# Graph attention layer on one core: TensorE's work of a step regrouped by operand type, the output projection's halves two steps apart, and counts of adj taken ahead of its transposes

## The reference

```python
h = max(layernorm(x), 0)                                   # (8, 1024, 64)
q, k, v = (h @ W + b).reshape(b, m, 8, 64)                 # 8 heads
scores = einsum(q, k) / 8 + edge_bias[adj]                 # (8, 8 heads, 1024, 1024)
scores = leaky_relu(scores, 0.2)
scores = where(adj > 0, scores, -1e9)
attn = softmax(scores, axis=-1)
out = einsum(attn, v).reshape(b, m, 512)
return x + out @ Wp + bp
```

## Time and profile before

| what | us |
|---|---|
| median of 3 runs (all: 1156.67, 1154.0, 1156.44) | 1156.44 |
| the profiled execution | 1153.11 |
| its span, first to last instruction | 1151.3 |
| PE busy in it (88%) | 1013.4 |
| DVE busy (81%) | 932.3 |
| ACT busy (67%) | 773.6 |
| POOL busy (42%) | 482.6 |

### The profile page before, as it was taken

How to read it: one execution, slowest core, us unless ns; L and a number is a source line. 1 busy time by engine, 2 the same in 40 slices (tenths; PEclk the granted TensorE clock), 3 DMA queues, 4 the chain that set the end, 5 groups by cost and what they waited for, 6 DMA issues and landing times. The chain is left out here.

```text
span 1151.3 us, 32436 instructions
## 1 busy us (share of the span) xinstructions
PE 1013.4 (88%) x9055; PEld 990.2 (86%) x9055; DVE 932.3 (81%) x3374; ACT 773.6 (67%) x1721; POOL 482.6 (42%) x865
## 2 busy tenths in 40 slices
PE   3247899999999999999989999999989999999996
PEld 3137898999989988989989989999989999899995
DVE  3725888978988879878898879978988789978984
ACT  1336776677767766767766767667777677667762
POOL 1001344444434544444444434444544355444444
PEclk9976999999999999999999999999999999999998
DMA  7183343433343343423434243433434243333220
GB/s 156 29 281 110 88 118 103 127 99 114 114 115 114 95 121 93 138 83 113 122 96 143 76 123 111 117 94 105 129 95 130 81 139 111 109 99 108 75 79 8
DMA packets 193427, 125.53 MB, mean 109 GB/s; under 512 B 34452, under 2 KB 181908, under 8 KB 193236
## 3 DMA queue, kind: packets, MB, share of 16 engines
q1 hardware_dynamic: 190736, 122.73, 37.2%
q10 hardware_dynamic: 2500, 0.55, 0.3%
HBM read 79.19 MB, written 44.04 MB: 107 GB/s over the span
## 5 line engine op out<-in xcount | busy, mean ns | idle before, releaser
L1007 POOL TENSOR_SCALAR a_line<-w,a_bias 128x256 f32<-128x256 f32 x512 | 260.3, 508 | 550.6 <-DVE w L1673 504.2
L1650 DVE CUSTOM_DVE_ANT_0 w<-bank,mask_rows 128x256 f32<-128x256 f32 x512 | 196.6, 421 | 119.3 <-PE bank L1140 96.3
L1426 ACT ACTIVATE pt<-bank 128x512 f32<-128x512 f32 x256 | 154.4, 603 | 183.7 <-PE bank L1150 178.7
L1197 PE MATMUL bank<-pt,nat_sb 128*65 128x128 f32 x2048 | 271.7, 277 | 0.2
L1197 PEld LDWEIGHTS bank<-pt,nat_sb 128*65 128x65 f32 x2048 | 237.4, 141 | 0.6 <-issue 0.6
L1673 DVE SCALAR_TENSOR_TENSOR w<-w,shift,a_line 128x256 f32<-128x256 f32 x512 | 224.1, 477 | 7.0 <-issue 4.9
L1662 DVE TENSOR_TENSOR onehot<-val,counts_to 128x512 fp32r<-128x512 f32 x256 | 175.3, 686 | 9.8 <-DVE val_max L1617 9.2
L1408 ACT ACTIVATE mask_own<-bank,mask_bias 128x512 bf16<-128x512 f32 x256 | 177.1, 692 | 2.1 <-PE bank L1174 2.1
L1150 PE MATMUL bank<-ident,w 128*128 128x128 f32 x1024 | 157.1, 277 | 0.0
L1417 ACT ACTIVATE t_sb<-bank 128x512 fp32r<-128x512 f32 x256 | 152.4, 595 | 4.6 <-PE bank L1162 4.5
L1139 PE MATMUL bank<-t_sb,q_hi 128*128 128x256 f32 x512 | 146.9, 308 | 5.3 <-issue 4.6
(11 more groups left out here) (132 smaller groups left out, 1654.2 us busy)
## 6 DMA issues: line engine op xcount, KB each, us to landing
adj_in<-in_adj_dram SPq DMA_DIRECT2D x64, 512.0 KB, 4.0
mask_store<-mask_own SPq DMA_DIRECT2D x64, 512.0 KB, 3.2
mask_rows<-mask_store SPq DMA_DIRECT2D x512, 64.0 KB, 2.4
stack_store<-stage SPq DMA_DIRECT2D x14, 256.0 KB, 3.1
h_stack<-stack_store SPq DMA_DIRECT2D x7, 512.0 KB, 5.2
h_nl<-nl_store SPq DMA_DIRECT2D x28, 128.0 KB, 3.0
x_res<-in_x_dram SPq DMA_DIRECT2D x16, 128.0 KB, 2.3
nl_store<-nl_rest SPq DMA_DIRECT2D x1, 2048.0 KB, 8.8
```

The source lines that it names most:

```text
L1007: nc.gpsimd.tensor_scalar(a_line[:, i % 2, :], w[:, i, :], 5.0, a_bias[:, i:i + 1], ALU.mult, ALU.add)\
L1197: last = pe.matmul(o_part[0:D + 1, P * u:P * u + P], nat_sb[:, t % 2, p % 4 * 2 + u, k, :], pt[:, p % 2, u, k, :], start=(k == 0), stop=(k ...
L1426: nc.scalar.activation(pt[:, p % 2], turned_bank[:, :].rearrange("p (u k r) -> p u k r", u=2, k=2), ACT.Exp, scale=0.8).then_inc(probs_rea ...
L1650: nc.vector.tensor_tensor_reduce(w[:, i, :], row_bank[:, SLOTS * u:SLOTS * u + SLOTS], mask_rows[:, t % 2, p % 4 * 2 + u, :], 0.25, LEAST_ ...
```

## The change

- The lags: `TURN_A` goes from 5 to 9 (still step 1), `COUNT` from 6 to 7 (step 2 to step 3), `USED` from 7 to 8 (step 3 to step 0), `PROJ` from 27 to 28, with its second half two steps after the first (steps 0 and 2, before 3 and 0), `NORM` from 28 to 29 with the same distance (steps 1 and 3, before 0 and 1), `SUM` from 30 to 32 (step 2 to step 0), `OUT` from 31 to 33.
- PE's step: `project`, `turn_adj` and `count` come right behind `weigh` and ahead of `gather_keys`; before, they came behind `natural`, in the order `turn_adj`, `count`, `project`. The wait for `adj_ready` moves from `turn_adj` to `count`, which is now the first reader of a tile of `adj`.
- VectorE's step: `flag_used` comes ahead of `take_scores`; the subtraction at the end of a graph runs a step after `take_ranks`' lag.
- GpSimd's `convert` waits for `a_turned` of the tile two before as well.

```diff
--- before.py
+++ after.py
@@ -40,9 +40,9 @@
     RING = 8
     PARTS = ((0, 8), (8, 32), (32, 64))
 
-    LOAD, CONV, TURN_A, COUNT, USED, RANK, VAL, ONEHOT = 0, 4, 5, 6, 7, 8, 9, 9
+    LOAD, CONV, COUNT, USED, RANK, TURN_A, VAL, ONEHOT = 0, 4, 7, 8, 8, 9, 9, 9
     MASK, MASK_OUT, TFILL, QFILL, BETA, COLSUM, VEC = 10, 14, 13, 9, 6, 18, 22
-    SCORE, A_LINE, Y, TURN, PV, X_ADD, PROJ, NORM, SUM, OUT = 17, 19, 20, 21, 22, 24, 27, 28, 30, 31
+    SCORE, A_LINE, Y, TURN, PV, X_ADD, PROJ, NORM, SUM, OUT = 17, 19, 20, 21, 22, 24, 28, 29, 32, 33
     K0 = 32
 
     x_tiles = x.rearrange("b (t p) d -> p (b t) d", p=P)
@@ -291,6 +291,9 @@
                     return t, f
             return None
 
+        def proj_piece(b, s):
+            return piece(b, s, PROJ, 2, 2)
+
         def q_piece(b, s, lag):
             for i in range(4):
                 y = every(b, s, lag + 2 * i, 8)
@@ -980,6 +983,7 @@
                 pool.wait_ge(adj_landed[t % 2], 16 * (MT * b + t // 2 + 1))
                 if later(n, 2):
                     pool.wait_ge(cnt_done, n - 1)
+                    pool.wait_ge(a_turned, n - 1)
                 pool.nop(nofuse=True)
                 nc.gpsimd.tensor_scalar(adj_bf[:, t % 2, :], adj_in[:, t % 2, :], 1.0, 0.0, ALU.mult, ALU.add)\
                     .then_inc(adj_ready, 1)
@@ -1094,7 +1098,7 @@
                 t = tile(b, s, COUNT)
                 if t is not None:
                     yield cnt_ready, TPG * b + t + 1
-                due = piece(b, s, PROJ, 2)
+                due = proj_piece(b, s)
                 if due is not None:
                     yield proj_taken, 2 * (TPG * b + due[0]) + due[1] + 1
 
@@ -1199,7 +1203,6 @@
                 last.then_inc(pv_done, 1)
 
             def turn_adj(b, t, s):
-                pe.wait_ge(adj_ready, TPG * b + t + 1)
                 free(adj_bank_uses, b, s, 0)
                 for k in range(TPG):
                     last = pe.transpose(adj_bank[:, :].bitcast(BF16)[:, P * k:P * k + P], adj_bf[:, t % 2, P * k:P * k + P],
@@ -1208,6 +1211,7 @@
 
             def count(b, t, s):
 
+                pe.wait_ge(adj_ready, TPG * b + t + 1)
                 free(adj_bank_uses, b, s, 0)
                 for k in range(TPG):
                     last = pe.matmul(adj_bank[:, GPT * k:GPT * k + GPT], adj_bf[:, t % 2, P * k:P * k + P], groups[:, :],
@@ -1239,6 +1243,15 @@
                 p = pair(b, s, PV)
                 if p is not None:
                     weigh(b, p)
+                due = proj_piece(b, s)
+                if due is not None:
+                    project(b, *due, s)
+                t = tile(b, s, TURN_A)
+                if t is not None:
+                    turn_adj(b, t, s)
+                t = tile(b, s, COUNT)
+                if t is not None:
+                    count(b, t, s)
                 due = piece(b, s, TFILL, 4)
                 if due is not None:
                     gather_keys(b, *due)
@@ -1248,15 +1261,6 @@
                 p = pair(b, s, SCORE)
                 if p is not None:
                     natural(b, p)
-                t = tile(b, s, TURN_A)
-                if t is not None:
-                    turn_adj(b, t, s)
-                t = tile(b, s, COUNT)
-                if t is not None:
-                    count(b, t, s)
-                due = piece(b, s, PROJ, 2)
-                if due is not None:
-                    project(b, *due, s)
                 i = 0
                 t = tile(b, s, RANK)
                 if t is not None:
@@ -1675,19 +1679,21 @@
                 t = tile(b, s, COUNT + 1)
                 if t is not None:
                     take_counts(b, t)
+                t = tile(b, s, USED)
+                if t is not None:
+                    flag_used(b, t)
                 p = pair(b, s, SCORE)
                 if p is not None:
                     for u in range(2):
                         take_scores(b, p, u)
-                t = tile(b, s, USED)
+                t = tile(b, s, VAL + 1)
                 if t is not None:
-                    flag_used(b, t)
                     if t % TPG == TPG - 1:
 
                         dve.wait_ge(adj_copied, TPG * b + t + 1)
                         cols = square_sums_adj[:, bass.ds(TPG * b + t - TPG + 1, TPG)]
                         nc.vector.tensor_tensor(cols, cols, cnt_sums[:, :], ALU.subtract).then_inc(kinds_noted, 1)
-                due = piece(b, s, NORM, 2)
+                due = piece(b, s, NORM, 2, 2)
                 if due is not None:
                     norm(b, *due)
                 t = tile(b, s, VAL)
```

## The result

The changed kernel is slower: 1214.01 us (median of 4 runs) against 1156.56 us of the kernel before on the same chip, ratio 1.050 with a 95% interval of 1.0474 to 1.0527. The prediction had the direction and missed the size: 1165 forecast, 1143 to 1190 as its range, and the kernel lies 24 us above the upper end.

The account below looks back on a forecast made before the run. PE was taken to be bound by waits for DVE, above all `rank` for `q_lo`. Plain periods +0.6 and special -0.3 gave +1.2 a graph, +9 over eight; 1153.1 + 9 + 3.3 = 1165 us, range 1143 to 1190.

Parts of the forecast that it names:

- the two new waits: PE in steps 1 and 3: `turn_adj` and `count` wait for `norm` on DVE, 0.6 and 0.57 us.
- The counts: Step 3: `count` waits for `norm` of the second half until 2.36 us; PE is there at 1.8.
- Step 2 and its special items: Step 2 takes 3.6 us against 2.85; with an extra item, 1.04 idle for `q_lo` goes, some 1.2 with latency.
- Step 0: Period's first step: `rank` waits for `q_lo`, free at 3.7; step ends at 3.8 us against about 4.35 before.
- the 0.3 given back in half of the periods: Special periods, four of eight a graph: 0.3 us back because DVE's lateness behind `beta` meets a PE waiting twice.
- a rival with a chance of 0.17: Step 0: `add_heads` starts before `shift_neg`, both shifts long, +0.4 a period, 1190; 0.17 shared with `x_res` at its median.
- The chain with short shifts: DVE in step 0, `take_scores` to `q_lo` without long shifts: 1.60 us, so `rank` is free at 3.31.
- The small terms: Among them, scores and `q` behind f32r instead of bf16: 0.1 us less in a plain period.
- Step 1: With the wait of `turn_adj` for `norm`, the step takes 4.4 us against 3.72; bounds 4.35 and 5.0.
- step 3: With the wait of `count` for `norm`, the step takes 4.0 us against 4.16.
- Type order: PE's operand type changes, 17 to 12 a period: worth nothing; rival at 0.09 each 1136, chance 0.18 with unseen gains.
- The periods with beta: `beta_pick` on DVE makes `q` and then step 0 late, as before the change; put at nothing.

Follow-up runs that it names:

- e9: The changed kernel with only `turn_adj` (step 1) put back behind `natural`: 1168.46 us, ratio 1.010 to the kernel before.
- e10: The changed kernel with only `count` (step 3) put back behind `natural`: 1204.65 us, ratio 1.0436 to the kernel before.
- e1: The changed kernel with GpSimd's `add_heads` ahead of its two `a_line` operations in a step: 1223.95 us, ratio 1.054 to the kernel before.
- e5: The changed kernel with `add_heads` ahead of `a_line` and `convert` one step earlier: 1185.35 us, ratio 1.026 to the kernel before.
- e11: e7 with `project` alone put behind `weigh`, ahead of `gather_keys`: 1099.33 us, ratio 0.953 to the kernel before.
- e6: The changed kernel with `q_lo` right behind `take_scores` in VectorE's step 0, ahead of the shifts: 1179.95 us, ratio 1.020 to the kernel before.
- e2: The changed kernel's lags, with `project`, `turn_adj` and `count` behind `natural` again: 1166.02 us, ratio 1.0047 to the kernel before.
- e7: The changed kernel with the edits of e2 and e6 together: 1095.47 us, ratio 0.947 to the kernel before.

## Why the prediction missed

- **Direction and the two new waits: right.** "`turn_adj` needs the bank that `project` filled in step 0, so `norm` of the first half, and DVE runs that in step 1": forecast at 2.5 us of the step, measured 2.52 in the period shown (635.75 - 633.23) and 2.59 at the median. The counts: forecast 2.36, median 2.45. e9 shows the price of the first, 46 us where the forecast had 0.68 a period, 41 us. e10 got back only 9 us for the second, as `rank` and the clock took the rest.
- **Step 2 and its special items: right.** 3.6 forecast, 3.52 measured, and hardly a wait for `q_lo` there.
- **Step 0: the step that failed.** "I take one of the two as long, 3.7": `rank` came at 4.19 at the median and 4.42 in the mean. Step 0 was to be 0.55 shorter than before, which with the 0.3 given back in half of the periods is 0.40 in the mean; it is 0.12 longer. 0.52 x 60 is 31 of the 49 us by which the forecast was low. In its place both shifts are long: each waits for the GpSimd operation that it meets. The mechanism was named as a rival with a chance of 0.17, and it was decided by an order of 0.1 us between two engines that came out of an estimate of how far VectorE runs ahead. The estimate was 0.2 us off and the order turned: `add_heads` starts before `shift_neg` in 46 of 61 periods, and in the 14 with `beta` it is `convert` that `shift_neg` meets.
- **The price of that rival was too low as well.** It took the `shift_neg` of step 2 (0.53 us), but what a shift costs is what is left of the GpSimd operation that it meets: 0.67 here, 0.99 for `shift` in e1. So `rank` came at 4.19 where the rival had 4.03. The chain with short shifts was low too: 1.60 takes off the length of `o_all`, 0.41, where the next operation starts 0.33 behind it, so it is 1.68; the 24 periods of e5 with both shifts short have 1.72.
- **The small terms.** The 0.1 a period that was taken off for scores and `q` behind f32r did not come: the score block of step 3 takes 0.56 behind `natural`, as it did behind `count` before, and `q` of step 1 takes 0.56 behind `natural`, as it did behind `turn_adj`. Since `natural` is f32r itself, it isn't the type ahead that makes a score block 0.08 longer than behind `q` (0.48). Step 1 cost 0.80 and not 0.68, and step 3 saved 0.10 and not 0.16, since `q` takes 0.56 and not 0.48. Together these are some 16 us more, most of what step 0 leaves.
- **Type order.** That a change of type has no price was drawn from one place without a gap; step 2 of e11 bears it out for f32 and f32r.
- **The periods with beta.** `rank` comes at 5.09 us in the 14 of 61 periods behind `beta_pick`, at 4.22 in the rest. But before the change it was late there too, 4.64 against 4.20. So the change adds 0.45 in 14 periods, 6 us, and the 0.3 that the forecast gave back in half of the periods was enough for it.
- **The range** took 0.4 us a period as the price of the rival. At its measured price step 0 is 0.54 longer than forecast (4.34 against 3.8, median), 32 us, and the small terms are 16: 1165 + 32 + 16 = 1213. The range left out that they can come together.

## What to carry to other kernels

Before a block is moved earlier in an engine's list, look up which buffer it waits for and where its consumer stands in the same step: grouping work by kind gained nothing here, since two of the moved blocks then waited for an engine that didn't come earlier. For a wait of one engine for another, look at where in its list the awaited engine does the awaited thing, and whether it can do it sooner: e6's edit is four lines, and together with e2's it makes the changed lags pay. And where two engines meet by a margin of a tenth of a microsecond, both outcomes belong in the range at their full price.

## What was not expected of the hardware

- VectorE operations that read and write only SBUF can be held by a GpSimd operation under way. Those of 4 columns end with it: `shift` took 0.15 us alone, 0.42 at the median beside the adds (58 in the trace after), 0.99 beside `convert` (37 in e1). `w` (128x256) took 0.68 and up to 0.96 beside the adds against 0.48 (e1). Operations with an input from PSUM beside the same GpSimd work kept their length: `q_lo` 0.47 us (113 beside the adds, after), `take_scores` 0.42 (88 beside `convert`, after).
- TensorE's granted clock fell to the lower level (1.2 GHz) while TensorE was busy for 88% of the span (e2), often at `rank`'s waits of 0.7 to 1.4 us, and the 3.4 us that followed cost some 1.6 us. Where `rank`'s wait went, these falls went too: 22 in e2, 4 in e7. Waits at another place didn't bring them: e6 has 43.1 and 24.9 us of waits ahead of the transposes and the counts, of up to 1.4 and 0.5 us, and 4 falls. So the price of a wait in this kernel isn't linear: of two `beta` periods of e2 in a row, from `rank` to `rank`, the one ahead of the fall shown took 17.17 us (707.83 to 725.00) and the one with it 18.91 (to 743.91). Why a wait at `rank` brings a fall at one time and not at another stays open.
